# Weighting expert outputs where they are made, and adding them to the residual by DMA, in a two-layer graph attention and mixture-of-experts kernel

## The chip, the cores and the metric

One Trainium2 chip, one of its cores. The metric is the device time of one execution in microseconds, as the median of several runs. In the trace PE is TensorE's matmul, PEld its weight load, DVE is VectorE, ACT is ScalarE, POOL is GpSimd and SP is SyncE; a q behind a name (SPq, ACTq) is that engine's instruction queue.

## The reference

128 graphs of 64 nodes, D = 256, so 8192 tokens. Two layers, each a graph attention and a mixture of 8 experts of which each token uses 2:

```python
# layer 0
x = x + gnn0(layernorm(x), adj)        # Wh = h @ W; e = a1.Wh + a2.Wh; masked softmax; attention @ Wh; elu
t = layernorm(x)
probs = softmax(t @ router_w.T); rw, re = top_k(probs, 2); rw = rw / rw.sum()
x = x + t + sum_k rw[k] * (gelu(t @ w1[re[k]] + b1[re[k]]) @ w2[re[k]] + b2[re[k]])    # hidden 256
# layer 1
x = x + gnn1(layernorm(x), adj)        # the same with a leaky relu ahead of the mask
t = layernorm(x)
vals, idx = top_k(t @ Wg + bg + bias, 2); w = softmax(vals)
x = x + sum_k w[k] * (relu(t @ W1[idx[k]] + b1[idx[k]]) @ W2[idx[k]] + b2[idx[k]])     # hidden 512
```

## The kernel before

Tokens are held in SBUF as `X`, 64 tiles of 128 tokens by 256 values in f32, through both graph layers. Each engine has its program written out in the order in which it runs; waits are on semaphores that count, and a wait holds everything behind it on its engine.

**Graph layer** (both layers). Eight groups g of eight tiles. TensorE turns x (`turn_x`, line 731, a quarter q of a group at a time, two tiles), multiplies by W (`project`, L743) into two banks in turn (2 and 3), builds the edge scores (`edges`, L750, L751), turns the softmax (`turn_probs`, L761) and multiplies by it (`attend`, L771). ScalarE copies the turned x (`copy_xT`, L972), scales the projected rows by 1/std (`scale_rows`, L981), and does the exponentials (L1003, L1019). VectorE does the softmax (`soft`, which starts at L1297), `add_relu` (L1321), `add_exp` (L1328) and the statistics of the result (`second_stats`, L1230), and it prepares group g+2 inside group g. TensorE projects group g+1 inside group g.

**Layer 0's input statistics** are bn_stats (`first_stats`) and a few small steps (`first_norm`); GpSimd takes the inverse root.

**Layer 1's input** is made from layer 0's outputs. GpSimd gathers, for each tile and each of its two choices, the expert's output rows from `yslots` in HBM into a ring (`gather_outputs`, L576, 128 indirect DMAs into `ring0` in WREG; from tile 16 on each pair of tiles waits until TensorE has turned the tile 16 back). VectorE multiplies each by the token's gate and adds it to X (`add_outputs`, L1240, 128 operations, the second with the row sum), and makes the negative mean (L1248). ScalarE makes the sum of squares (`squares`, L997), and VectorE the inverse root (`first_rstd`, L1277 to L1286). In the same groups ScalarE and GpSimd cut layer 1's weights into two f16 parts (L1025, L1026, `low_part` L590).

**Tokens and router.** ScalarE normalises (L1096), VectorE and GpSimd cut the tokens into two f16 halves (L1417, L628), SyncE stores them to HBM: in layer 0 to `split_tokens`, 1024 bytes a row; in layer 1 to `token_rows`, rows of 2056 bytes with tokens, x and two gates. TensorE makes the logits.

**Routing.** VectorE ranks tokens by expert and finds each one's slot. To invert this, it builds one-hot matrices of lane and block for 16 token and choice pairs at a time (L1576 to L1590, `lane_hot`, `block_hot`, the 16 pairs side by side for each lane), and TensorE multiplies them (L890), reading each pair's columns 32 bytes apart. `gather_row` (L1627) is the result, and GpSimd's gathers wait for it. In layer 1 ScalarE then stores the gates at the rows' ends (L1161, 8 bytes for each token). In layer 0 ScalarE adds token and residual meanwhile (x_plus_y, L1138).

**Expert slots.** 256 rows a slot, 68 slots in layer 0 (four of them mixed, with two experts), 2 x 36 in layer 1. In slot s, by engine:

```python
# TensorE                       # ScalarE              # VectorE
output(s)        # L940         activate(s + 2)        cut_hidden(s + 1)   # L1644, L1646
turn_over(s + 3) # L909         # L1149                copy_out(s)         # L1656, waits for output(s)
hidden(s + 2)    # L926                                copy_T(s + 3)       # L1638
```

GpSimd gathers the rows (L640 in layer 0, four slots ahead), and in layer 0 SyncE stores each slot's output to `yslots` when `copy_out` is done. Layer 1 multiplies its outputs by the gate in the slot already (L1669), and its second pass scatters rows to the output (L667). The slots run as a loop of four (layer 0) with the experts' addresses in registers.

## Time and profile before

| | us |
|---|---|
| median of 3 runs | 1438.54 (1426.94 to 1439.29) |
| profiled execution, whole | 1430.36 |
| its span, first to last instruction | 1428.6 |
| busy: TensorE, VectorE, GpSimd, ScalarE | 1123.7, 964.8, 705.0, 551.0 |
| mean granted TensorE clock | 0.856 |

The profile is of one execution. Busy time of an engine says little by itself; what matters is what each stage waits for. By the trace the stages are: graph layer 0 to 186 us, tokens to 240, routing to 296, slots to 538 (layer 0); graph layer to 811, tokens to 862, routing to 930, first pass to 1171, second to the end (layer 1).

### The profile page before, as it was taken

Reading aid. Unit: us, or ns where it says so; the run is one execution under the profiler, and the core shown is the slowest. Engines: PE = TensorE matmul, PEld = TensorE weight load, DVE = VectorE, ACT = ScalarE, POOL = GpSimd, SP = SyncE. Lnnn points to the kernel's source line nnn. Section 1 sums busy time; section 2 is a strip of 40 time slices with the busy share of each in tenths; the row PEclk is TensorE's granted clock in tenths of the full one; section 3 lists DMA queues with packets and bytes.
Section 4 is the critical chain, followed back from the end, with each engine's and each line's share of the span. In section 5 each row is a group of like instructions: output and inputs, shape, how many; then the busy total and the mean of one; then the engine's idle time right before and its main releaser. Section 6 shows DMA issues by size and latency. Waiting matters only on the chain.

```text
span 1428.6 us, 31605 instructions
## 1 busy us (share of the span) xinstructions
PE 1123.7 (79%) x9392; PEld 910.2 (64%) x9393; DVE 964.8 (68%) x1844; ACT 551.0 (39%) x1229; POOL 705.0 (49%) x752
## 2 busy tenths in 40 slices
PE   5988765669999991577667487769999997889995
PEld 4766554348888871355455373549889885668884
DVE  3888688937777762458887797827767664556663
ACT  2646475712222221566766484012222221212221
POOL 3565864045555527756670280045433115677762
PEclk9999855559999995788998658579999998989998
DMA  9211133025555544235452553447766624344430
GB/s 279 55 45 38 60 124 112 1 63 163 162 162 160 165 119 129 85 83 145 123 150 61 147 177 118 3 133 216 201 178 193 147 91 126 111 132 127 124 112 12
DMA packets 126095, 172.53 MB, mean 121 GB/s; under 512 B 35109, under 2 KB 94000, under 8 KB 125744
## 3 DMA queue, kind: packets, MB, share of 16 engines
q0 software_dynamic: 28288, 83.03, 21.9%
q1 hardware_dynamic: 89504, 88.22, 20.0%
q10 hardware_dynamic: 8208, 0.07, 1.0%
q8 instruction: 53, 0.87, 0.3%
q14 instruction: 42, 0.34, 0.1%
HBM read 100.87 MB, written 71.44 MB: 121 GB/s over the span
## 4 chain that ended last, share of the span: by engine, by line
PE 55%; issue 19%; DVE 11%; POOL 6%; ACT 3%; another core or an unknown queue 3%; DMA 2%; DVEq 1%; POOLq 0%; SPq 0%; ACTq 0%
PE bank L926 19%; PE bank L940 19%; PE bank L743 4%; PE bank L909 4%; PE bank L890 3%; DVE X L1240 2%; PE bank L771 2%; POOL arena L628 2%; DVE stats L1230 1%; ACT b_bc L997 1%; PE bank L750 1%; DMA X<-first_rows,gather_row 1%; PE bank L751 1%; DVE X L1321 1%
## 5 line engine op out<-in xcount | busy, mean ns | idle before, releaser
L1149 ACT ACTIVATE arena<-bank,b1T 128x256 f32<-128x256 f32 (+1 forms) x464 | 176.2, 458 | 562.9 <-PE bank L926 363.2
L926 PE MATMUL bank<-arena,WREG 128*128 128x256 f16 (+1 forms) x2784 | 326.5, 270 | 28.2 <-issue 16.6
L940 PE MATMUL bank<-WREG,arena 128*128 x2544 | 304.9, 275 | 21.2 <-issue 13.9
L926 PEld LDWEIGHTS bank<-arena,WREG 128*128 x2784 | 253.8, 99 | 70.7 <-issue 40.4
L940 PEld LDWEIGHTS bank<-WREG,arena 128*128 128x128 f16 x2544 | 246.9, 99 | 61.1 <-issue 29.6
L1644 DVE CAST arena<-arena 128x1024 f16<-128x1024 f32 (+1 forms) x140 | 82.3, 588 | 187.2 <-ACT arena L1149 145.9
L640 POOL DMA_INDIRECT arena<-split_tokens,gather_row x136 | 129.9, 955 | 152.3 <-PE bank L909 64.4
L743 PE MATMUL bank<-wg_sb,arena 128*128 128x258 f32 x512 | 141.6, 423 | 57.6 <-issue 19.7
L576 POOL DMA_INDIRECT WREG<-expert_outputs,pos_both x128 | 126.6, 989 | 91.2 <-issue 35.5
L650 POOL DMA_INDIRECT X<-token_rows,gather_row x72 | 72.5, 1006 | 180.5 <-DMA first_rows<-X 95.9
L743 PEld LDWEIGHTS bank<-wg_sb,arena 128*128 128x128 f32 x512 | 102.4, 209 | 82.4 <-issue 42.6
L1646 DVE TENSOR_TENSOR arena<-arena 128x1024 f16<-128x1024 f32 (+1 forms) x140 | 135.3, 966 | 4.8
L1656 DVE SCALAR_TENSOR_TENSOR arena<-bank,b_bc 128x512 f32<-128x512 f32 (+1 forms) x152 | 97.0, 644 | 37.7 <-PE bank L940 21.3
L1638 DVE COPY arena<-bank 128x1024 f16<-128x1024 f16 x140 | 95.4, 682 | 39.2 <-remote 25.5
L650 POOL DMA_INDIRECT X<-first_rows,gather_row x72 | 76.3, 1060 | 76.8 <-DMA first_rows<-X 47.5
L667 POOL DMA_INDIRECT out<-X,scatter_row x72 | 85.2, 1184 | 58.4 <-DVE X L1669 39.4
L628 POOL TENSOR_TENSOR arena<-arena 128x512 f16<-128x512 f32 x64 | 75.4, 1188 | 44.2 <-DVE arena L1417 44.2
L981 ACT ACTIVATE arena<-bank,minus_one,cols 128x258 f32<-128x258 f32 x128 | 71.1, 565 | 65.7 <-PE bank L743 26.9
L828 PE MATMUL bank<-ident,arena 128*128 128x128 f16 x512 | 65.1, 307 | 37.4 <-POOL arena L628 36.9
L771 PE MATMUL bank<-arena 128*128 128x256 f32 x256 | 73.2, 421 | 25.9 <-DVE X L1321 10.9
L1240 DVE SCALAR_TENSOR_TENSOR X<-WREG,cols,X 128x256 f32<-128x256 f32 x128 | 66.2, 580 | 26.4 <-DMA WREG<-expert_outputs,pos_both 20.6
L771 PEld LDWEIGHTS bank<-arena 128*128 128x128 f32 x256 | 53.3, 214 | 48.1 <-issue 30.2
(205 smaller groups left out, 1577.4 us busy)
## 6 DMA issues: line engine op xcount, KB each, us to landing
first_rows<-X SPq DMA_DIRECT2D x72, 257.0 KB
expert_outputs<-arena SPq DMA_DIRECT2D x68, 256.0 KB
X<-in_x SPq DMA_DIRECT2D x16, 512.0 KB
split_tokens<-arena SPq DMA_DIRECT2D x16, 512.0 KB, 2.9
stage_w<-in_L_ffn_W SPq DMA_DIRECT2D x16, 512.0 KB
token_rows<-X SPq DMA_DIRECT2D x8, 1024.0 KB
token_rows<-arena SPq DMA_DIRECT2D x16, 512.0 KB, 3.8
stage_w<-in_L_ffn_w SPq DMA_DIRECT2D x16, 256.0 KB, 2.7
```

The costliest lines, as they stand in the source:

```text
L576: nc.gpsimd.indirect_dma_start(out=ring0[:, o:o + D], out_offset=None, in_=yslots, in_offset=bass.IndirectOffsetOnAxis(ap=pos_i[k][:, t:t ...
L628: nc.gpsimd.tensor_tensor(y16_4[:, 2 * q:2 * q + 2, D:2 * D], y32_4[:, 2 * (q % 4):2 * (q % 4) + 2, :], y16_4[:, 2 * q:2 * q + 2, 0:D], AL ...
L640: nc.gpsimd.indirect_dma_start(out=gat[:, u * 512:(u + 1) * 512], out_offset=None, in_=table, in_offset=bass.IndirectOffsetOnAxis(ap=gathe ...
L650: nc.gpsimd.indirect_dma_start(out=token_row(ST * j + a, 0, ROW), out_offset=None, in_=first_rows if f else token_rows, in_offset=bass.Ind ...
L743: last = mm(bank[2 + t % 2][:, 0:WA], xT[:, b:b + P], wg(L, c, 0, WA), start=c == 0, stop=c == KC - 1)
L771: last = mm(bank[6 + q % 2][:, a * D:(a + 1) * D], probsT[:, j * P:(j + 1) * P], Wh[g % 2][:, j * WA:j * WA + D], start=True, stop=True)
L926: last = mm(hb, w1_at(L, ea, wh, kc, fc), tT[:, tb:tb + width], start=n == 0, stop=n == 3 * KC - 1)
L940: last = mm(ob[a], hsrc[:, h0:h0 + P], w2_at(L, e[a % len(e)], wh, fc), start=fc == 0 and n == 0, stop=fc == FC - 1 and n == 2)
L1149: ins = A(hid[:, h0:h0 + width], bank[2 + 2 * (u % 2) + fc // 2][:, b0:b0 + width], ACT.Gelu if L == 0 else ACT.Relu, bias=cut(b1T, ea * F ...
L1638: V.tensor_copy(tT[:, (u % 2) * 4 * SLOT:(u % 2 + 1) * 4 * SLOT], bank[u % 2][:].bitcast(F16)).then_inc(T_ev[L], 1)
L1646: tt(hid_lo[:, hb:hb + FC * SLOT], hid[:, hb:hb + FC * SLOT], hid_hi[:, hb:hb + FC * SLOT], ALU.subtract).then_inc(h_split[L], 1)
L1656: ins = stt(o_sb[:, o0:o0 + width].rearrange("p (a d) -> p a d", d=D), bank[6 + u % 2][:, a * width:(a + 1) * width].rearrange("p (a d) -> ...
```

## The change

1. Layer 0's expert outputs are multiplied by their gate in the slot. The gates ride at the end of each token's row: `split_tokens` gets rows of 1032 bytes (256 f32-sized words of token, two gates), ScalarE stores the gates there, and layer 0's gathers wait for that store. In each slot ScalarE picks the gate of the right choice for each row (`pick_gates`) and multiplies the output rows in place (`weigh`); SyncE's store waits for `weigh`.
2. Layer 1's gathers of those outputs go straight to X with `compute_op=add` (`add_choice`), the second choice of a half group after the first has landed; the first choice of half h waits until TensorE has turned half h-4. `add_outputs` and `squares` go. Layer 1's statistics are taken as in layer 0, by bn_stats and `first_norm`, and VectorE's order in the groups becomes that of layer 0.
3. The one-hot matrices hold pairs side by side (two columns, not sixteen), so TensorE reads its columns 4 bytes apart. `gates_ready` comes after the second batch in layer 0 too.
4. The first five tiles of a graph layer are projected into five banks (`FIRST_BANKS`), and ScalarE copies all four quarters of x ahead of the first scaling (in layer 1 the first two quarters, then four scalings).

```diff
-                def gather_outputs(g):
-                    for t in range(g * GT, (g + 1) * GT):
-                        if t >= 2 * GT and t % 2 == 0:
-                            pool.wait_ge(xT_mm[1], at((t - 12) // 2 + 1))
...
+                def add_choice(k, h):
+                    landed = (first_added, both_added)[k][h % 2]
+                    if h >= 2:
+                        pool.wait_ge(landed, 64 * (h // 2))
+                    if k:
+                        pool.wait_ge(first_added[h % 2], 64 * (h // 2 + 1))
+                    elif h >= 4:
+                        pool.wait_ge(xT_mm[1], at(2 * (h - 3)))
+                    for t in range(4 * h, 4 * h + 4):
+                        nc.gpsimd.indirect_dma_start(
+                            out=xs(t), out_offset=None, in_=yslots,
+                            in_offset=bass.IndirectOffsetOnAxis(ap=pos_i[k][:, t:t + 1].bitcast(U32), axis=0),
+                            compute_op=ALU.add).then_inc(landed, 16)
...
+                    pool.wait_ge(x_plus_y[0], at(TILES // 8))
+                    add_choice(0, 0)
                     for g in range(GROUPS):
-                        gather_outputs(g)
+                        for h in range(2 * g, 2 * g + 2):
+                            if h + 1 < 2 * GROUPS:
+                                add_choice(0, h + 1)
+                            add_choice(1, h)
                         if g == 1:
                             one_hot_rows()
...
                 pool.wait_ge(slots_ready[L], at(1))
+                pool.wait_ge(gates_stored, 16 + 16 * L)
...
                     if u % ST == 0 and t >= SV:
                         pool.wait_ge(T_mm[0], at(t // ST - SU + 1))
+                        pool.wait_ge(picks_made, 2 * ST * (t // ST - SU + 1))
...
+                def pick_gates(s, u, i):
+                    def choice(k, a):
+                        return cut(chosen_by[k], ST * s + a, 1)
+                    loop_wait(act, gathered[u % SU], i * (16 * ST) + 16 * ST * (u // SU + 1))
+                    for a in range(ST):
+                        r = u % SU * ST + a
+                        A(part[:, r:r + 1], gathered_row(r, D, 1), ACT.Identity, scale=choice(0, a)).then_inc(picks_made, 1)
+                    for a in range(ST):
+                        r = u % SU * ST + a
+                        loop_wait(act, picks_made, s * (2 * ST) + a + 1)
+                        A(picked[:, r:r + 1], gathered_row(r, D + 1, 1), ACT.Identity, scale=choice(1, a),
+                          bias=part[:, r:r + 1]).then_inc(picks_made, 1)
+                def weigh(s, u):
+                    loop_wait(act, o_ev[0], at(s + 1))
+                    loop_wait(act, picks_made, s * (2 * ST) + 2 * ST)
+                    for a in range(ST):
+                        r = u % SU * ST + a
+                        ins = A(o_sb[:, r * D:(r + 1) * D], o_sb[:, r * D:(r + 1) * D], ACT.Identity, scale=picked[:, r:r + 1])
+                    ins.then_inc(weighted[0], 1)
                 def slot(s, u, i, es):
+                    if L == 0:
+                        weigh(s, u)
                     if u + 2 < SLOTS[L]:
                         activate(s + 2, u + 2, es[2])
+                    if L == 0 and u + 3 < SLOTS[L]:
+                        pick_gates(s + 3, u + 3, i)
...
+FIRST_BANKS = (2, 3, 5, 6, 7)
+        def bank_of(t):
+            return FIRST_BANKS[t] if t < len(FIRST_BANKS) else 2 + t % 2
...
-                    pe.wait_ge(Wh_ev[L], at(t - 1))
+                    if bank_free(t):
+                        pe.wait_ge(Wh_ev[L], at(bank_free(t)))
...
-                        last = mm(bank[2][:, f * nt:f * nt + wide], lane_hot[g % 2].rearrange("p (l t) -> p t l", t=BATCH)[:, b, :],
-                                  block_hot[g % 2][:, 0:wide * BATCH].rearrange("p (l t) -> p t l", t=BATCH)[:, b, :],
+                        last = mm(bank[2][:, f * nt:f * nt + wide], hot(lane_hot[g % 2], P)[:, b // 2, :, b % 2],
+                                  hot(block_hot[g % 2], wide)[:, b // 2, :, b % 2],
```

On VectorE, the order of layer 1's groups:

```diff
                     if g:
-                        add_exp(L, g - 1, 2 + (L == 0))
+                        add_exp(L, g - 1, 3)
                     normalise_probs(L, g)
...
-                            for h in range(2):
-                                add_outputs(g + 2, h)
-                        add_relu(L, g, 0)
-                        add_relu(L, g, 1)
-                        add_exp(L, g, 0)
-                        add_relu(L, g, 2)
-                        add_exp(L, g, 1)
+                    if ahead:
+                        first_stats(L, g + 2, 0)
+                    add_relu(L, g, 0)
+                    add_exp(L, g, 0)
+                    if ahead:
+                        first_stats(L, g + 2, 1)
+                    add_relu(L, g, 1)
+                    add_exp(L, g, 1)
+                    if ahead:
+                        first_norm(L, (g + 2) * GT, GT)
...
+                    add_relu(L, g, 2)
+                    add_exp(L, g, 2)
```

## Rows read from the trace of the kernel before

**Rows 1.** Busy time by stage (stretch, length, engines, granted clock, DMA share, GB/s).

```profile
core 0: us, PE busy (x) PEld busy (x) DVE busy (x) ACT busy (x) POOL busy (x), PEclk, DMA share, GB/s
...
296.00:538.00 242.00, 218.97 (x2224) 192.64 (x2224) 164.91 (x277) 59.60 (x145) 129.67 (x136) 0.95 0.51 149
538.00:811.00 273.00, 160.60 (x800) 117.47 (x800) 184.20 (x489) 152.55 (x371) 148.81 (x138) 0.81 0.41 111
```

**Rows 2.** The same view for 25 slots of layer 0 and one group of layer 1.

```profile
320.00:400.00 80.00, 77.34 (x799) 68.95 (x797) 59.77 (x100) 20.86 (x50) 47.21 (x50) 1.00 0.56 161
655.70:681.50 25.80, 18.92 (x103) 14.35 (x103) 22.96 (x61) 18.34 (x45) 18.00 (x17) 0.93 0.52 143
```

**Rows 3.** Timeline of layer 0's slots, ScalarE and VectorE (start, duration, instruction, idle before).

```profile
403.17 0.84 ACT L1149 ACTIVATE arena<-bank,b1T 128x256 f32<-128x256 f32 x2 [2.10 <-issue]
...
401.78 0.69 DVE L1646 TENSOR_TENSOR arena<-arena 128x512 f16<-128x512 f32 x1
402.39 0.68 DVE L1656 SCALAR_TENSOR_TENSOR arena<-bank,b_bc 128x512 f32<-128x512 f32 x1
...
404.04 0.43 DVE L1644 CAST arena<-arena 128x512 f16<-128x512 f32 x1 [0.37 <-ACT arena L1149]
```

**Rows 4.** Timeline, VectorE: first and last softmax of each layer.

```profile
32.31 0.69 DVE L1297 SCALAR_TENSOR_TENSOR arena<-no_edge,bank 128x512 f32<-128x512 uint8 x1 [10.69 <-PE bank L751]
...
161.34 0.68 DVE L1297 SCALAR_TENSOR_TENSOR arena<-no_edge,bank 128x512 f32<-128x512 uint8 x1
...
594.19 0.69 DVE L1297 SCALAR_TENSOR_TENSOR arena<-no_edge,bank 128x512 f32<-128x512 uint8 x1 [7.78 <-issue]
...
785.95 0.69 DVE L1297 SCALAR_TENSOR_TENSOR arena<-no_edge,bank 128x512 f32<-128x512 uint8 x1 [1.88 <-PE bank L751]
```

**Rows 5.** Groups by line in 655.7 to 681.5 us (count, busy, mean ns, idle before).

```profile
L1240 DVE SCALAR_TENSOR_TENSOR X<-WREG,cols,X 128x256 f32<-128x256 f32 x16 | 8.8, 605 | 0.1
...
L1230 DVE BATCH_NORM_STATS2 stats<-X 128x6 f32<-128x256 f32 x8 | 2.7, 411 | 0.0
...
L997 ACT ACTIVATE b_bc<-X,cols 128x256 f32<-128x256 f32 x8 | 3.9, 496 | 0.0
```

**Rows 6.** Timeline, ScalarE: x_plus_y of layer 0, and the token stage's start in layer 1.

```profile
245.31 31.62 ACT L1138 ACTIVATE X<-X,cols  x64 [0.35 <-issue]
...
811.15 4.04 ACT L1096 ACTIVATE arena<-X,cols 128x256 f32<-128x256 f32 x8 [1.21 <-DVE ex L1404]
```

**Rows 7.** Timeline, start of layer 1: the eighth gather and VectorE's first addition.

```profile
546.76 0.95 POOL L576 DMA_INDIRECT WREG<-expert_outputs,pos_both  x1 [0.30 <-issue]
...
549.60 2.19 DVE L1240 SCALAR_TENSOR_TENSOR X<-WREG,cols,X 128x256 f32<-128x256 f32 x5 [13.54 <-DMA WREG<-expert_outputs,pos_both]
```

**Rows 8.** Single lines: ns min/median/max, first and last start.

```profile
L576 POOL DMA_INDIRECT WREG<-expert_outputs,pos_both x128: 942/948/1372, 538.0 to 745.6; - x128
...
L667 POOL DMA_INDIRECT out<-X,scatter_row x72: 982/1026/1721, 1196.9 to 1419.2; - x72
...
L1240 DVE DVE_READ_ACCUMULATOR X<-WREG,cols,X x64: 78/82/86, 551.7 to 757.4; 128x1 f32 x64
```

**Rows 9.** Groups by line, whole span (count, busy, mean ns, idle before).

```profile
L667 POOL DMA_INDIRECT out<-X,scatter_row x72 | 85.2, 1184 | 58.4 <-DVE X L1669 39.4 <-issue 18.9
...
L1576 DVE TENSOR_TENSOR arena<-arena,lane_of 128x2048 bf16<-128x2048 bf16 x16 | 19.6, 1223 | 5.4 <-PE bank L890 5.3
...
L590 POOL TENSOR_TENSOR WREG<-stage_w,WREG 128x1024 f16<-128x1024 f32 x8 | 17.0, 2131 | 38.7 <-ACT stage_w L1026 38.6
```

**Rows 10.** Routing: matmuls of layer 1, first gather of layer 0, the gates' store.

```profile
907.98 2.43 PE L890 MATMUL bank<-arena 128*128 128x72 bf16 x16 [0.18 <-DVE arena L1583]
911.37 17.32 PE L890 MATMUL bank<-arena 128*128 128x144 bf16 x64 [0.96 <-DVE arena L1590]
...
295.78 1.19 POOL L640 DMA_INDIRECT arena<-split_tokens,gather_row  x1 [63.16 <-DVE gather_row L1627]
...
token_rows<-cols ACTq DMA_DIRECT2D x1, 64.0 KB, 15.3
```

**Rows 11.** Timeline, ScalarE: the first scaling of layer 0.

```profile
19.76 1.02 ACT L981 ACTIVATE arena<-bank,minus_one,cols 128x258 f32<-128x258 f32 x2 [7.92 <-POOL cols L538]
```

More of the change, by code:

```diff
@@ L163, in build @@
         squared = [b2_bc[:, k * D:(k + 1) * D] for k in range(4)]
-        ring0 = WREG[:, 4 * 8 * HID[1]:].bitcast(F32)
+        chosen_by = [stats[:, k * STILES[0]:(k + 1) * STILES[0]] for k in range(TOPK)]
         y32 = carve(8 * D, 0)
@@ L1155, in slot @@
                     if u + 2 < SLOTS[L]:
                         activate(s + 2, u + 2, es[2])
-                if L == 1:
-                    act.wait_ge(gates_ready[1], at(1))
-                    with nc.allow_non_contiguous_dma(reason="two gates at the end of each token's row"):
-                        act.dma_start(rows_of()[:, :, 2 * D:ROW], gates[:].rearrange("p (t k) -> p t k", k=TOPK)).then_inc(gates_stored, 16)
-                act.wait_ge(slots_ready[L], at(1))
+                    if L == 0 and u + 3 < SLOTS[L]:
+                        pick_gates(s + 3, u + 3, i)
@@ L1163, in _ @@
+                act.wait_ge(gates_ready[L], at(1))
+                rows_here, last_column = (rows_of(), 2 * D) if L else (table.rearrange("(t p) c -> p t c", p=P), D)
+                with nc.allow_non_contiguous_dma(reason="two gates at the end of each token's row"):
+                    act.dma_start(rows_here[:, :, last_column:last_column + TOPK], gates[:].rearrange("p (t k) -> p t k", k=TOPK)).then_inc(gates_stored, 16)
+                act.wait_ge(slots_ready[L], at(1 if L else 2))
                 first = of_slots(act, slot_expert, L, phase(0, L, 2), 1)
@@ L1165, in _ @@
                     activate(s, s, first[s])
+                if L == 0:
+                    for s in range(3):
+                        pick_gates(s, s, 0)
                 all_slots(act, L, slot_expert, 1, 2, slot)
@@ L1265, in first_norm @@
                 ch.wait()
-                v, r = (one(n, g * GT, GT) for n in ("var", "rstd"))
+                v, r = (one(name, first, n) for name in ("var", "rstd"))
                 ch.mark(ts(c, c, 1.0 / D, EPS, ALU.mult, ALU.add))
```

222 lines of the change are left out of this document (94 added, 128 removed).

## The prediction

> **What bounds the kernel now.** I read the stage table first [rows 1]. TensorE is busy 218.97 of 242 us in layer 0's expert slots and only 160.60 of 273 in layer 1's graph layer. The change touches both, and the routing of each layer, so each is read by what it waits for.
>
> The slots of layer 0: 80 us hold 799 matmuls at 32 a slot, so 25 slots of 3.2 us, TensorE 77.34 us busy [rows 2]. ScalarE works 0.84 us a slot, then waits for `hidden`. VectorE's order is cast and subtraction (`cut_hidden` of the next slot), `copy_out`, `copy_T` [rows 3].
>
> The graph layer of layer 1: its eight softmaxes start from 594.19 to 785.95, 27.4 us apart on average, against 32.31 to 161.34 in layer 0, 18.4 us [rows 4]. In one group (25.80 us) VectorE is busy 22.96, ScalarE 18.34, GpSimd 18.00, TensorE 18.92 [rows 2]: VectorE is the bound, and its largest row there is `add_outputs`, 8.8 us [rows 5]. VectorE takes group g+2's tokens in its queue inside group g, so late tokens also hold the relu and exp steps queued behind them.
>
> **Part A, weighting in the slots (layer 0).** ScalarE gets, per slot, `weigh` (two 128x256 multiplies in place) ahead of `activate(s+2)`, and `pick_gates(s+3)` (four one-column operations) behind it. It has the room, but the new waits close a ring. `weigh(s)` waits for `copy_out(s)`; `activate(s+2)` is queued behind `weigh(s)`; `cut_hidden(s+2)` waits for `activate(s+2)`; `copy_out(s+1)` is queued behind `cut_hidden(s+2)` on VectorE; `weigh(s+1)` waits for it. One turn is one slot. Its terms: `weigh` 2 x 31.62/64 = 0.99, from layer 0's own x_plus_y of the same shape [rows 6]; `activate` 0.84; to VectorE 0.03 (404.01 to 404.04), and as much back; cast 0.43 and 0.03 to the next; subtraction 0.61 (401.78 to 402.39); `copy_out` 0.68 [rows 3]. Sum 3.64 us; the loop's hop, which falls on every fourth slot, is hidden only in part, so I take 3.75. Against 3.2 that is 0.55 x 64 = 35 us; four mixed slots and the tail (the last store waits for `weigh`) add 2, and the first slots, at half clock, where TensorE is slower than the ring, take 2 off: 35. Low end: `weigh` as short as `activate`'s two, no hop, 3.5, +19. High end: a further 0.1 us at each of the four hand-overs inside the ring, 4.05, +54. `copy_T`, the gathers (four slots ahead) and the stores are off the ring. TensorE then idles 0.5 us a slot; its clock was 1.00 at 97% busy and 0.93 at 73% [rows 2], so a loss from that belongs to the high end. The gathered rows grow from 1024 to 1032 bytes, beside a DMA share of 0.56 [rows 2]: nothing.
>
> **Part B, gathers that accumulate (layer 1).** VectorE loses 8.8 us a group and gains eight bn_stats, 2.7 for eight [rows 5]; the small steps around both about cancel. 6.1 of 22.96 us go, and 3.9 of ScalarE's (`squares`) [rows 5]. VectorE falls under 17, ScalarE to 14, TensorE's 19 stands. What is late next is GpSimd's queue: 16 gathers at 1.25 us and a `low_part` of 2.13 make 22.1 us a group [rows 7, 9]. The stage then follows from that queue: its start at 538.0 [rows 8], 128 gathers at c each, five `low_part` (10.7), `one_hot_rows` about 1, landing 1.9 (the eighth gather ends at 547.7, VectorE starts at 549.60 [rows 7]); then what follows the last tokens: now 757.4 to 811.15, 53.8 us [rows 6, 8], and some 50 with the lighter queues, since the rest of group 5, group 6 and group 7 remain. End = 601.6 + 128 c, against 811.15. The new waits add little: `add_choice(1, h)` waits for transfers issued 4 gathers (5 us) earlier that land in 1.9; the hold by `xT_mm` needs half h-4 turned, and the 16 gathers between that turn and the landing of half h take about as long as the group that lies between. The mean clock was 0.81 in the stage [rows 1], lowest at its beginning, where a slow first group holds the queue; I add 5 us for it.
>
> No row shows c, an accumulating gather. The gather into WREG is 0.95 + 0.30 = 1.25 us [rows 7]; the scatter, the other indirect transfer, has a median of 1.026 and a mean of 1.18, so 1.33 to 1.49 [rows 8, 9]. For less than 1.25 nothing speaks: the issue is the same GpSimd work with one operation more. I take 1.34, since a transfer that also has to read its target is nearer to the scatter. That ends at 773, 38 us earlier, less 5: 33 us. With 1.25 it is 45, with 1.49 14.
>
> The DMA engines: a share of 0.52 over 25.80 us moved 143 GB/s, 3.6 us per MB, so 0.48 us for a gather of 0.131 MB [rows 2]; twice that is still under c, and the sum keeps GpSimd's price. The Trainium skill, "DMA: Bandwidth & Descriptors", section "Rules for kernel authors", says that an accumulating DMA reads its destination and writes it later; a third pass over the bytes by that rule would make some 0.7 of the 0.48, no change of the sum, but it speaks for the rival on this price. No run so far shows such a transfer.
>
> **Part C, routing.** Lanes and blocks lie as pairs, so TensorE reads its moving columns 4 bytes apart and not 32. Now 64 matmuls of 144 columns take 17.32 us and 16 of 72 take 2.43: 0.271 and 0.152 us each, 1.65 ns a column, two cycles at half clock [rows 10]. VectorE waits 5.3 us for them in all [rows 9], and some 2.7 more at the ends of the two chains. If the column price halves, VectorE bounds; its operations keep size and type. In layer 0 the gathers now also wait for the gates' store, which ScalarE issues only after x_plus_y (276.9) and which took 15.3 us [rows 6, 10]: 292.3 against 295.78 now, 3 us at most after one for the new steps. With 3.6 in layer 1 I take 6.6, and 0 or -1 if the stride isn't the reason. The Trainium skill, "SBUF — State Buffer", section "Door 1: The DMA port swizzle", gives SBUF 16-byte lines and a penalty for every access to a new one; by it a 4-byte step is nearly free, which makes the same 6.6. The trace agrees for the 32-byte step, with its 1.65 ns.
>
> **Part D, five banks first.** TensorE can project five tiles before the first `scale_rows`, which starts at 19.76 in layer 0 [rows 11]; today the softmax follows at 32.31, with scaling and projection taking turns. Eight scalings back to back with three projections left save 3 us, or 0 if the next groups absorb it. In layer 1 it is inside the 5 us above.
>
> **Sum.** 35 - 33 - 6.6 - 3 = -7.6 on the profiled execution's 1430.36 us: 1422.8. The median of the three runs lies 8 us above that execution; I carry half of it and predict 1427.
>
> **Rivals.** (1) The accumulating gather is dear, and this one ends slower: c = 1.75. GpSimd's queue then holds the graph layer until 601.6 + 224 = 825.6, 14.5 us later than now, plus 5, plus 35 - 9.6: +45, 1475. It decides from the point where 35 - 9.6 + 5 - (209.6 - 128 c) passes 14 us, c = 1.51. For it: each transfer must fetch its target first; against: the scatter's price is 1.33. (2) The ring doesn't bind, because the weighing or the hand-overs are shorter, or the slots slip past each other: cost 5, total -38, 1393. For it: 3.64 is only 0.44 above the period; against: its terms are measured rows. (3) The change doesn't do what it says: the graph layer's pace stays near 25 us, since another chain through the in-order queues holds it, so B brings 10 and the total is +15, 1446. For it: ScalarE and TensorE idled 7 us a group too; against: VectorE 89% busy, and layer 0's 18.4 us.
>
> **Chances.** Forecast 0.45 (its own range 1400 to 1448, as c goes from 1.25 to 1.49 and the ring from 3.5 to 3.9), dear gather 0.22, no ring 0.19, no gain in the graph layer 0.14. The range 1387 to 1474 takes in rivals 2 and 3 and c up to 1.7. Within 1% (14 us, about what three runs that lie 12 us apart can tell) lie 0.24 of the forecast's share and 0.02 of rival 3's; faster has 0.17 and rival 2's 0.19; slower has the rest.
>
> **What would show it.** In the profile after: slots of 3.7 to 3.8 us in layer 0, with `weigh` waiting for VectorE and the cast waiting for ScalarE; if they keep 3.2, part A's ring is wrong. The start-to-start spacing of the accumulating gathers is c. Softmaxes of layer 1 22 to 25 us apart with GpSimd hardly idle; if they are 18 to 20 apart, GpSimd isn't the bound. Routing batches without VectorE's waits for TensorE. The prediction is wrong above all if c lies outside 1.25 to 1.5, or if the lighter load of TensorE in the slots brings the clock down.

## The result, and the profile after

The changed kernel takes 1486.2 us (median, 1483.1 to 1491.8) beside 1438.1 for the kernel before on the same chip: a ratio of 1.037, 95% interval 1.032 to 1.042, slower. The profiled execution took 1491.78 us (span 1490.0, mean clock 0.854), 61.4 more than that of before.

Both traces, cut at the same marks (the first gather of layer 0's slots, the first gather of expert outputs, the first normalisation of layer 1's tokens, the first gather of layer 1's slots), lengths in us:

| stage | before | after | |
|---|---|---|---|
| up to layer 0's first gather | 295.8 | 288.7 | -7.1 |
| slots of layer 0 | 242.2 | 275.3 | +33.1 |
| graph layer of layer 1 | 273.2 | 304.5 | +31.3 |
| tokens and routing of layer 1 | 119.0 | 114.3 | -4.7 |
| the two passes of layer 1 | 498.5 | 507.3 | +8.8 |

The busy time by stage, as in [rows 1], cut at the marks of after:

```profile
core 0: us, PE busy (x) PEld busy (x) DVE busy (x) ACT busy (x) POOL busy (x), PEclk, DMA share, GB/s
288.70:563.90 275.20, 227.47 (x2224) 188.40 (x2224) 161.54 (x277) 179.71 (x553) 128.73 (x136) 0.97 0.45 132
563.90:868.40 304.50, 166.11 (x800) 120.00 (x800) 148.28 (x392) 122.45 (x243) 220.36 (x138) 0.76 0.55 100
```

In the slots ScalarE rose from 59.60 to 179.71 us, and no engine is full; the granted clock was 0.97, against 0.95 before, so the lighter load of TensorE cost no clock. In the graph layer VectorE fell by 36 us and ScalarE by 30, as meant, but GpSimd rose by 72, and the layer got longer with it.

**The slots.** The ring is the circle of waits between ScalarE and VectorE that part A describes. The timeline that answers to [rows 3], ScalarE and then VectorE. L1191 is `weigh`, L1166 `activate`, L1178 and L1182 the picks, L1675 and L1677 `cut_hidden`, L1687 `copy_out`; an arrow in brackets names what ended the wait:

```profile
423.74 0.91 ACT L1191 ACTIVATE arena<-arena 128x256 f32<-128x256 f32 x2 [1.13 <-DVE arena L1687]
424.55 0.81 ACT L1166 ACTIVATE arena<-bank,b1T 128x256 f32<-128x256 f32 x2
425.26 0.47 ACT L1178 ACTIVATE arena<-arena,stats 128x1 f32<-128x1 f32 x2
425.68 0.66 ACT L1182 ACTIVATE arena<-arena,stats 128x1 f32<-128x1 f32 x2
427.32 0.91 ACT L1191 ACTIVATE arena<-arena 128x256 f32<-128x256 f32 x2 [0.98 <-DVE arena L1687]
...
422.87 0.68 DVE L1687 SCALAR_TENSOR_TENSOR arena<-bank,b_bc 128x512 f32<-128x512 f32 x1
...
425.40 0.43 DVE L1675 CAST arena<-arena 128x512 f16<-128x512 f32 x1 [1.25 <-ACT arena L1166]
425.86 0.69 DVE L1677 TENSOR_TENSOR arena<-arena 128x512 f16<-128x512 f32 x1
426.47 0.68 DVE L1687 SCALAR_TENSOR_TENSOR arena<-bank,b_bc 128x512 f32<-128x512 f32 x1
```

The ring can be walked: `copy_out` starts at 422.87, `weigh` at 423.74 behind it, `activate` at 424.55 behind that, the cast at 425.40, `copy_out` again at 426.47. One turn is 3.60 us; the turns alternate between 3.60 and 3.74, from the third slot to the mixed ones, 3.67 on average over 48 slots. Before, TensorE set them, at 3.07 to 3.45, 3.24 on average. So the ring costs 0.43 x 64 = 28 us of the 33.1. Of the rest, 2.1 us are a pause at 505 us, 1.1 the tail behind the last `copy_out`, and 1.7 the first slots. Both traces have a pause of some 7 us there. In the kernel before it lies ahead of the first `copy_out` (22.1 us behind the stage's first gather, where the other chip below has 15); in the changed kernel it lies between the first `copy_out` and the second, 11.4 us apart, where the run without the hold, on that other chip, has 5.0. The pause itself is thus no price of the change. VectorE's timeline of before, and TensorE's of after, in which the matmuls of one slot come singly:

```profile
308.39 0.69 DVE L1638 COPY arena<-bank 128x1024 f16<-128x1024 f16 x1 [6.50 <-remote]
```

```profile
312.75 0.39 PE L975 MATMUL bank<-WREG,arena 128*128 x2 [1.93 <-issue]
313.35 0.37 PE L975 MATMUL bank<-WREG,arena 128*128 x1 [0.21 <-issue]
314.08 0.38 PE L975 MATMUL bank<-WREG,arena 128*128 x1 [0.36 <-issue]
```

The waits of the stage (total, times, longest) show the ring as well:

```profile
ACT arena L1191 <- DVE arena L1687: 74.0, 66, 4.9
DVE arena L1675 <- ACT arena L1166: 72.2, 57, 2.0
```

**The graph layer.** The accumulating gathers as one line, what GpSimd waited for ahead of them, who waited for them, and their landing:

```profile
L601 POOL DMA_INDIRECT X<-expert_outputs,pos_both x128: 1540/1540/1957, 563.9 to 811.8; - x128
its engine sat idle before it (us, times) until:
  issue: 36.8, 123
  DMA expert_outputs<-arena: 22.8, 1
  DMA X<-expert_outputs,pos_both: 1.2, 4
who waited for it (us, times):
  DVE stats L1278: 139.5, 15
...
DMA to landing us min/median/max: 3.7/3.8/4.6
```

And in GpSimd's timeline, with starts 1.84 to 1.85 us apart:

```profile
573.24 1.54 POOL L601 DMA_INDIRECT X<-expert_outputs,pos_both  x1 [0.30 <-issue]
575.09 1.54 POOL L601 DMA_INDIRECT X<-expert_outputs,pos_both  x1 [0.30 <-issue]
576.93 1.54 POOL L601 DMA_INDIRECT X<-expert_outputs,pos_both  x1 [0.30 <-issue]
```

So c, the prediction's price of one accumulating gather on GpSimd, is 1.54 + 0.30 = 1.845 us by the starts, where the plain gather into WREG had 1.25 [rows 7, 8]. GpSimd waited 1.2 us in all for landings and never for TensorE's turns of the half that is to be overwritten (the hold): it costs nothing here. VectorE's bn_stats waited 139.5 us for the tokens. The softmaxes that answer to the second half of [rows 4] start at 634.87 and 844.30, 29.9 us apart on average, against 27.4:

```profile
634.87 0.69 DVE L1330 SCALAR_TENSOR_TENSOR arena<-no_edge,bank 128x512 f32<-128x512 uint8 x1
...
844.30 0.69 DVE L1330 SCALAR_TENSOR_TENSOR arena<-no_edge,bank 128x512 f32<-128x512 uint8 x1
```

**Routing and first group.** The rows that answer to [rows 10], [rows 11] and the first of [rows 4], in the timelines, and the gates' store in the list of DMA issues:

```profile
961.86 1.14 PE L925 MATMUL bank<-arena 128*128 128x72 bf16 x16 [2.41 <-DVE arena L1609]
...
971.23 2.10 PE L925 MATMUL bank<-arena 128*128 128x144 bf16 x16 [1.28 <-DVE arena L1616]
...
19.20 2.85 ACT L1018 ACTIVATE arena<-bank,minus_one,cols 128x258 f32<-128x258 f32 x6
...
28.53 0.69 DVE L1330 SCALAR_TENSOR_TENSOR arena<-no_edge,bank 128x512 f32<-128x512 uint8 x1 [7.46 <-PE bank L783]
```

```profile
split_tokens<-cols ACTq DMA_DIRECT2D x1, 64.0 KB, 12.8
```

A matmul of 144 columns takes 2.10/16 = 0.131 us, half of the 0.271 of before, and TensorE waits for VectorE between the batches, while VectorE's 5.3 us of waits for these matmuls are gone. Layer 0's first softmax comes 3.8 us earlier, and the scalings ahead of it run six in a row.

### The profile page after: what moved, and what is told of

The parts are those of the page before. It is cut to its first block, busy times and chain, and to the rows that moved or that the text cites. A ratio compares the mean times of both kernels' runs of the same rounds, so it can differ in the third digit from the quotient of the medians.

```text
span 1490.0 us, 32667 instructions
## 1 busy us (share of the span) xinstructions
PE 1107.3 (74%) x9392; PEld 898.8 (60%) x9393; DVE 924.7 (62%) x1750; ACT 640.2 (43%) x1509; POOL 770.0 (52%) x752
## 3 DMA queue, kind: packets, MB, share of 16 engines
q0 software_dynamic: 40576, 83.17, 24.9%
## 4 chain that ended last, share of the span: by engine, by line
PE 33%; issue 25%; POOL 16%; DVE 13%; ACT 4%; DMA 3%; another core or an unknown queue 2%; ACTq 1%; DVEq 1%; SPq 1%; POOLq 0%
PE bank L975 13%; PE bank L961 13%; POOL X L601 10%; DVE arena L1687 3%; ACT arena L1166 2%; PE bank L944 2%; PE bank L775 2%; POOL arena L658 2%; DVE arena L1675 1%; DMA X<-expert_outputs,pos_both 1%; DVE arena L1601 1%; DVE stats L1278 1%; POOL WREG L615 1%; ACT arena L1191 1%
## 5 line engine op out<-in xcount | busy, mean ns | idle before, releaser
L975 PE MATMUL bank<-WREG,arena 128*128 x2544 | 308.3, 274 | 57.0 <-issue 25.8
L1166 ACT ACTIVATE arena<-bank,b1T 128x256 f32<-128x256 f32 (+1 forms) x464 | 174.4, 453 | 408.9 <-PE bank L961 276.2
L975 PEld LDWEIGHTS bank<-WREG,arena 128*128 128x128 f16 x2544 | 241.7, 98 | 110.7 <-issue 82.2
L1675 DVE CAST arena<-arena 128x1024 f16<-128x1024 f32 (+1 forms) x140 | 82.7, 591 | 250.1 <-ACT arena L1166 203.7
L601 POOL DMA_INDIRECT X<-expert_outputs,pos_both x128 | 199.6, 1559 | 60.8 <-issue 36.8
L1278 DVE BATCH_NORM_STATS2 stats<-X 128x6 f32<-128x256 f32 x256 | 87.6, 410 | 140.7 <-DMA X<-expert_outputs,pos_both 139.5
L775 PE MATMUL bank<-wg_sb,arena 128*128 128x258 f32 x512 | 139.5, 419 | 31.5 <-ACT arena L1018 27.8
L1677 DVE TENSOR_TENSOR arena<-arena 128x1024 f16<-128x1024 f32 (+1 forms) x140 | 135.3, 966 | 4.8
L803 PE MATMUL bank<-arena 128*128 128x256 f32 x256 | 76.3, 436 | 46.1 <-DVE X L1354 43.4
L1687 DVE SCALAR_TENSOR_TENSOR arena<-bank,b_bc 128x512 f32<-128x512 f32 (+1 forms) x152 | 96.6, 642 | 17.1 <-remote 11.0
L803 PEld LDWEIGHTS bank<-arena 128*128 128x128 f32 x256 | 53.9, 218 | 70.8 <-issue 60.4
L1191 ACT ACTIVATE arena<-arena 128x256 f32<-128x256 f32 x136 | 61.7, 500 | 75.9 <-DVE arena L1687 74.0
L1048 ACT ACTIVATE arena<-bank,plus_one 128x512 f32<-128x512 f32 x64 | 43.9, 686 | 116.0 <-PE bank L803 112.0
```

The costliest lines, as they stand in the source:

```text
L601: nc.gpsimd.indirect_dma_start(out=xs(t), out_offset=None, in_=yslots, in_offset=bass.IndirectOffsetOnAxis(ap=pos_i[k][:, t:t + 1].bitcast ...
L775: last = mm(Wh_bank(t), xT[:, b:b + P], wg(L, c, 0, WA), start=c == 0, stop=c == KC - 1)
L803: last = mm(bank[6 + q % 2][:, a * D:(a + 1) * D], probsT[:, j * P:(j + 1) * P], Wh[g % 2][:, j * WA:j * WA + D], start=True, stop=True)
L975: last = mm(ob[a], hsrc[:, h0:h0 + P], w2_at(L, e[a % len(e)], wh, fc), start=fc == 0 and n == 0, stop=fc == FC - 1 and n == 2)
L1166: ins = A(hid[:, h0:h0 + width], bank[2 + 2 * (u % 2) + fc // 2][:, b0:b0 + width], ACT.Gelu if L == 0 else ACT.Relu, bias=cut(b1T, ea * F ...
L1278: ch.mark(V.bn_stats(stats[:, t * 6:(t + 1) * 6], xs(t)))
```

## The experiments

The runs came onto several chips, of two kinds: on one kind the kernel before takes 1438 to 1445 us, as in the first pair of traces, on the other 1368 to 1369. I call them the slower and the faster chip and compare within one kind. A difference between two chips of one kind is less sure than one within a chip, and is named where it is used. Stage lengths in us from the profiles, one execution each, cut as above:

| kernel | chip | first gather | slots | graph layer 1 | routing 1 | passes of 1 |
|---|---|---|---|---|---|---|
| before | slower | 295.8 | 242.2 | 273.2 | 119.0 | 498.5 |
| changed | slower | 288.7 | 275.3 | 304.5 | 114.3 | 507.3 |
| changed, again | slower | 289.1 | 277.3 | 302.6 | 115.7 | 509.4 |
| second choice accumulates | slower | 288.0 | 275.8 | 271.5 | 114.0 | 506.5 |
| half rows, half columns | slower | 288.1 | 277.3 | 296.1 | 116.9 | 506.6 |
| activate first, no picks | slower | 288.8 | 247.6 | 304.8 | 114.2 | 510.4 |
| before | faster | 297.6 | 231.9 | 263.0 | 119.0 | 460.0 |
| no hold | faster | 288.2 | 265.8 | 302.9 | 115.6 | 459.4 |
| activate first | faster | 289.4 | 245.4 | 302.8 | 115.6 | 458.6 |
| plain gathers | faster | 287.8 | 265.8 | 230.1 | 114.1 | 456.6 |
| routing and banks | faster | 289.5 | 231.8 | 259.9 | 115.1 | 456.5 |
| routing and banks, again | faster | 288.9 | 232.3 | 258.5 | 115.2 | 457.2 |
| weights in slots, plain sum | faster | 287.6 | 236.0 | 246.0 | 114.4 | 453.7 |
| plain sum without weights in slots | faster | 286.9 | 232.2 | 251.3 | 114.3 | 460.3 |

**1. The order in the slot.**

```diff
+                    if u + 2 < SLOTS[L]:
+                        activate(s + 2, u + 2, es[2])
                     if L == 0:
                         weigh(s, u)
-                    if u + 2 < SLOTS[L]:
-                        activate(s + 2, u + 2, es[2])
```

> The changed kernel, with activate(s+2) ahead of weigh(s) in ScalarE's slot of layer 0. Theory (the ring of weigh, activate, cast, subtraction and copy_out sets 3.65 us a slot): activate no longer stands behind weigh, so the ring is open and a slot goes back to TensorE's 3.2 us; layer 0's slots take some 245 us instead of 275.3, and the whole is 26 to 32 us shorter than the changed kernel, about 1457. Rival (the slots are longer because ScalarE, GpSimd or the transfers of 1032-byte rows have more to do, whatever their order): the slots keep 3.5 us or more, and the whole moves by less than 10 us.

Measured: 1410.8 us, ratio to the kernel before 1.032 (1.025 to 1.038). On this chip the changed kernel stands in the run without the hold (1433.4): 22.6 us less, and 20.4 less in the slots (245.4 against 265.8). The `copy_out`s come no longer evenly but 3.82, 3.77, 3.22, 2.67 us apart, 13.4 for four, where the same chip needs 12.75 without weighting. So the order was most of the price, as the theory said, but 13.5 us stayed against the kernel before on a chip of this kind (231.9). In the steady slots, which hold most of them, one wait of TensorE's comes in four slots, for nothing that the profile shows: 1.03 us here, where the same wait of the kernel before is 0.30. TensorE's timeline:

```profile
409.52 1.47 PE L961 MATMUL bank<-arena,WREG 128*128 128x256 f16 x12
412.02 1.15 PE L975 MATMUL bank<-WREG,arena 128*128 x9 [1.03 <-issue]
```

**2. Without the picks as well.**

```diff
-                        pool.wait_ge(picks_made, 2 * ST * (t // ST - SU + 1))
...
-                    if L == 0 and u + 3 < SLOTS[L]:
-                        pick_gates(s + 3, u + 3, i)
...
-                        ins = A(o_sb..., o_sb..., ACT.Identity, scale=picked[:, r:r + 1])
+                        ins = A(o_sb..., o_sb..., ACT.Identity, scale=plus_one[:])
```

> The changed kernel with activate(s+2) ahead of weigh(s), and without pick_gates: weigh multiplies by 1 in place, so the gates are left out; GpSimd's gathers no longer wait for the picks. With activate first the slots took 13.4 us for four, against 12.7 without any weighting, and TensorE stood still once in four slots for 1.0 us. Theory (ScalarE's slot, 0.84 + 0.90 + 1.0 us with the loop's hop on top, comes late once in four slots, and the picks fill it): without them four slots take 12.7 to 12.9 us, and the whole is 10 us or more below activate first, 32 or more below the changed kernel. Rival (the wait comes from the hand-overs of TensorE itself or of weigh): four slots keep 13.2 us or more.

Measured on the slower chip: 1465.3 us, 28.7 below the changed kernel beside it (1494.0), ratio 1.014 (1.009 to 1.019). Four slots take 13.1 us, where the kernel before needs 12.9 on this chip and the changed one 14.7, so the ring and nearly all of the rest are gone. Both figures missed what I expected, 12.7 to 12.9 and 32 us, which came from the other chip. The picks, four operations on one column, about 1.1 us a slot, were the second part of the price. The edit also takes away the gathers' wait for the picks, so the two are not separated. How they come to hold TensorE once in four slots, the trace doesn't show.

**3. The price of the gather.** The first of two edits of the same line, all gathers plain:

```diff
-                            in_offset=bass.IndirectOffsetOnAxis(ap=pos_i[k][:, t:t + 1].bitcast(U32), axis=0),
-                            compute_op=ALU.add).then_inc(landed, 16)
+                            in_offset=bass.IndirectOffsetOnAxis(ap=pos_i[k][:, t:t + 1].bitcast(U32), axis=0)).then_inc(landed, 16)
```

> The changed kernel, with the 128 gathers of layer 1 as plain gathers into X at the same place, under the same waits: they overwrite X, so the addition to the residual is left out. Theory (the accumulating gather costs GpSimd 1.845 us where a plain one costs 1.25): the spacing falls to 1.25 us, the graph layer of layer 1 to between 225 and 245 us from 304.3, and the whole is 60 to 80 us shorter than the changed kernel, about 1416. Rival 1 (the layer is held by the order, the hold on TensorE's turns, half after half, and by the landing): spacing within a half falls, the layer keeps over 290 us. Rival 2 (the price is that of writing into X at all, 1 KB apart in each partition, not of the accumulation): the spacing stays near 1.8 us.

Measured: 1359.8 us, ratio 0.994 (0.992 to 0.997), 73.7 below the run without the hold. The line of the gathers:

```profile
L601 POOL DMA_INDIRECT X<-expert_outputs,pos_both x128: 942/946/1402, 553.6 to 728.8; - x128
```

The same place in X, the same waits, the same rows: 0.946 us, and the graph layer takes 230.1 where it took 302.9. Both rivals fall: neither the order nor the writing into X is the price, the accumulation is. The prediction's line, 63.6 us (601.6 less its start at 538.0) + 128 c, and its 5 us more for the start, give 228.6 for c = 1.25, 1.5 us under the 230.1 measured.

**4. Half of them.** `compute_op` only where k is 1.

> The changed kernel, in which the first choice's gathers are plain and overwrite X, so the residual is left out, and only the second choice's accumulate. Theory (the graph layer of layer 1 ends with GpSimd's queue, a straight line in the mean price of a gather): the mean is (1.25 + 1.845) / 2 = 1.55 us, so 128 x 0.30 = 38 us are gone from the graph layer, to about 266 us, and the whole is 34 to 40 us below the changed kernel. Rival (each second-choice gather waits for the first choice's landing, or the layer falls at once to the pace of VectorE and TensorE): less than 25, or more than 55 us.

Measured: 1459.6 us, 34.4 below the changed kernel, the graph layer 271.5 us, 31.1 shorter. The mean busy time of its gathers, by the groups of the stage:

```profile
L601 POOL DMA_INDIRECT X<-expert_outputs,pos_both x128 | 165.2, 1291 | 60.7 <-issue 37.4 <-DMA expert_outputs<-arena 22.7 <-PE bank L762 0.6
```

With the 0.30 to the next that is a mean c of 1.59, a little over the 1.55 expected, and 128 x (1.845 - 1.59) = 33 us by the line, 31.1 measured. This kernel's graph layer is about as long as that of before (273.2): part B breaks even there at c = 1.6, and it cost 1.845. On the faster chip, where before's layer takes 263.0, the same line breaks even at 1.52.

**5. What the price depends on.** The first choice's gathers with rows of 512 bytes (L602), the second choice's with 64 rows of 1024 (L607), in one execution.

```diff
+                        if k == 0:
+                            ... out=xs(t)[:, 0:D // 2], in_=yslots.rearrange("r (two c) -> (r two) c", two=2), ...
+                        else:
+                            ... out=xs(t)[0:P // 2, :], ap=pos_i[k][0:P // 2, t:t + 1] ...
```

> The changed kernel with halved accumulating gathers: the first choice's fetch 128 rows of 512 bytes, the second choice's 64 rows of 1024 bytes, so both move half the bytes; half of the expert outputs are left out. Theory (GpSimd's price lies in what it writes for each row): 128 rows of half the width keep 1.54 us busy, 64 whole rows fall to between 0.8 and 1.1. Rival (the price lies in the bytes, in a queue that pushes back): both fall to the same. Second rival (a fixed price of the instruction): both keep over 1.4.

Measured, in GpSimd's timeline:

```profile
592.65 1.54 POOL L602 DMA_INDIRECT X<-expert_outputs,pos_both  x1 [0.30 <-issue]
594.50 1.42 POOL L607 DMA_INDIRECT X<-expert_outputs,pos_both  x1 [0.30 <-issue]
596.22 1.42 POOL L607 DMA_INDIRECT X<-expert_outputs,pos_both  x1 [0.30 <-DMA X<-expert_outputs,pos_both]
```

My theory was wrong: half the bytes cost the same 1.54, as it said, but half the rows 1.42 and not 0.8 to 1.1. The second rival holds. An estimate from the two: 1.9 ns for a row and 1.30 us whatever the size; so a smaller accumulating gather saves next to nothing. The mean c is 1.48 + 0.30 = 1.78, for which the line gives 296.4 us of graph layer with the 5; 296.1 were measured.

**6. Without the hold.**

```diff
-                    elif h >= 4:
-                        pool.wait_ge(xT_mm[1], at(2 * (h - 3)))
```

> The changed kernel without the wait of the first choice's half h for TensorE's turn of half h-4. Theory (GpSimd's queue is the bound and never waits there): no change, within 3 us of the changed kernel. Rival (the hold delays the first choice and so all of the queue): 10 us or more shorter.

Measured on the faster chip: 1433.4 us, ratio 1.047 (1.041 to 1.052), with a graph layer of 302.9 us. The run with `activate` first, on the same chip and with the hold, has 302.8. The hold costs nothing.

The ratio is higher than the changed kernel's 1.037, but the stages don't show it. From the table, the graph layer costs 39.9 us on this chip and 31.3 on the slower one, where before's is 10 us longer and GpSimd's price is not; the passes cost nothing here and 8.8 there; the slots cost 33.9 and 33.1. In sum the spans differ by 60.4 and 61.4 us. The medians differ by 64.3 and 48.0, so the ratio's difference lies between single executions and medians.

**7. The changed kernel again.**

> The changed kernel as it is, so that the next three have it beside them on one chip. Theory: its graph layer of layer 1 takes 303 to 305 us, its slots hold 3.60 to 3.75 us, and it is 55 to 65 us longer than the kernel before; where the two passes of layer 1 took 8.8 us longer in the first profile, with no line of them changed, they now take the same as in the other kernels of the chip.

Measured: 1494.0 us, 48.6 above the kernel before (1445.4), ratio 1.033 (1.028 to 1.038), with a graph layer of 302.6 us. The 55 to 65 was read off two single executions; the first one of before had been 8 us under its median. The graph layer and the ring repeat as expected. The passes of layer 1 did not fall back to those of before: all five traces of changed kernels on this kind of chip have 506.5 to 510.4 us there, the one trace of before 498.5; on the faster chip all kernels have 453.7 to 460.3, before among them with 460.0. So on the slower chip the 8.8 us come back each time, with no line of the passes changed, and on the faster one they are absent. Their cause stays open. What the slower chip has and the faster one lacks are pauses whose releaser the profile calls remote: they stand in each of its traces, of before too, and in none of the faster chip's. Some come at the same place in each, the first slots of layer 0 and the start of each pass, with lengths that vary. First of before, then of after, by the waits of the whole span:

```profile
ACT arena L1149 <- remote: 47.6, 6, 12.0
```

```profile
ACT arena L1166 <- remote: 124.5, 10, 45.4
```

The pauses in the slots named above end with such waits as well (6.50 us of VectorE's before, 3.78 after). What they are, the trace doesn't say.

**8. Routing and banks alone.** The kernel before with part C, and part D in layer 0.

> The kernel before, with the pairwise one-hot matrices of both layers and the five banks and the copies first in layer 0; no weighting in the slots, no accumulating gathers. Theory (these parts gain what the two traces differ by in their stages, 3.8 at layer 0's start, 3.3 less the gates' store in its routing, 4.4 in layer 1's): 8 to 12 us shorter than the kernel before, about 1428. Rival (the differences of single stages come from elsewhere, and the later stages absorb them): within 3 us of the kernel before.

Measured: 1354.6 us, ratio 0.990 (0.987 to 0.992), 14.6 us below before, more than expected.

> The kernel before with pairwise one-hot matrices and layer 0's five banks, once more, so that it stands beside the version above on one chip: 0.9895 of the kernel before, 0.986 to 0.993. If the version above is right, it is 15 to 30 us shorter than this one.

Measured: 1354.7 us, ratio 0.991 (0.988 to 0.994), 15.3 us above the version below (1339.4). Beside it the kernel before was profiled, for its stages:

> The kernel before, for its stages on this chip. Theory: 12.9 to 13.0 us for four slots, its last stage (layer 1's two passes) within 3 us of that of the other two kernels here, so that the 8.8 us by which the first two traces differ there are a difference of runs and not of kernels. Rival: its last stage is 6 us or more shorter than theirs.

Measured: a span of 1371.5 us, its passes 460.0, within 3 us of the 457.2, but 6.3 above the 453.7 of the version below, and four slots in 12.75 us, under the 12.9 to 13.0 expected. Against it this kernel is 8.7 us earlier at the first gather, 4.5 shorter in the graph layer (of which 2.0 are GpSimd's two iotas, 5.2 us before and 3.2 now) and 3.8 in the routing of layer 1.

**9. A version from what was learned.** Plain gathers into the ring, weights in the slots with `activate` first and the picks on VectorE, and half by half one addition for each choice:

```diff
+                    for k in range(TOPK):
+                        o = (c % 4 * TOPK + k) * 4 * D
+                        ins = tt(xs(4 * c, 4), xs(4 * c, 4), ring0[:, o:o + 4 * D], ALU.add)
...
+                    tt(parts, both, cut(chosen_pairs, TOPK * ST * s, TOPK * ST)..., ALU.mult).then_inc(picks_made, 1)
+                    loop_wait(dve, picks_made, s * 2 + 1)
+                    tt(picked[:, r:r + ST], parts[:, :, 0], parts[:, :, 1], ALU.add).then_inc(picks_made, 1)
```

> A version made of what the runs so far showed. From the changed kernel: the weighting in the slots, pairwise one-hot matrices, five banks, bn_stats; with activate(s+2) ahead of weigh(s), and the picks as two small operations on VectorE behind copy_T. In layer 1 the gathers are plain, into the ring of the kernel before, and VectorE adds a half (four tiles, 128x1024) of each choice in one operation, which the weighting makes possible. Theory: four slots take 12.7 to 13.1 us; an addition of 128x1024 takes 1.1 to 1.3 us, four a group, 4.8 in place of 8.8 + 0 for squares, so VectorE has 16.9 + 4.8 = 21.7 us a group beside GpSimd's 22.1; the graph layer of layer 1 falls to 235 to 250 us, and the whole is 28 to 45 us below the kernel before, ratio 0.969 to 0.981. Rival (the stage needs both queues, and late tokens hold the relu and exp steps behind the additions as before): the graph layer keeps over 260 us, ratio 0.985 or more.

Measured: 1339.4 us, ratio 0.980 (0.977 to 0.982): below both kernels and clear of noise, 28.6 us under before. Four slots take 12.97 us, against 12.75; the slots as a whole 3.7 to 4.1 us more than without weighting, where the changed kernel paid 33. The graph layer takes 246.0. But the way there isn't the one expected. Its costliest groups of VectorE between 524 and 790 us:

```profile
L1262 DVE TENSOR_TENSOR X<-X,WREG 128x1024 f32<-128x1024 f32 x32 | 47.3, 1479 | 33.3 <-DMA WREG<-expert_outputs,pos_both 32.8
L1252 DVE BATCH_NORM_STATS2 stats<-X 128x6 f32<-128x256 f32 x128 | 44.1, 412 | 0.6
```

The statistics take 22 us more than before, and VectorE is busy 190.7 us in this stage, more than before's 183.9. ScalarE lost 30.7. The mean of an addition is 1.48 us and not 1.1 to 1.3, but 28 of the 32 took 1.21 to 1.23, as expected. The other four took 1.9, 3.0, 3.1 and 5.1, and each ran beside a `low_part` of GpSimd's (L614). The median, and the longest of them beside GpSimd:

```profile
L1262 DVE TENSOR_TENSOR X<-X,WREG x32: 1206/1225/5095, 535.2 to 717.9; 128x1024 f32<-128x1024 f32 x32
...
707.37 4.21 POOL L614 TENSOR_TENSOR WREG<-stage_w,WREG 128x1024 f16<-128x1024 f32 x2
707.58 5.09 DVE L1262 TENSOR_TENSOR X<-X,WREG 128x1024 f32<-128x1024 f32 x1
```

**10. Which half of it.** The same without weights in the slots, VectorE multiplying tile by tile:

> The version with the plain sum, without the weighting in the slots: no weigh, no picks, rows of 1024 bytes again, and in layer 1 VectorE multiplies by the gate in eight operations of 128x256 a half, as in the kernel before, but with bn_stats, the order of the relu and exp steps and the banks of the changed kernel. It asks where the 12.5 us came from by which the graph layer of the plain sum (246.0 us) was shorter than that of the kernel with routing and banks alone (258.5), since its two wide additions took 1.48 us each and VectorE was busy for 190.7 us, more than the 183.9 before. Theory A (the wide additions: 47.3 us in all against 66.3, and VectorE bounds the stage): the graph layer is 10 to 19 us longer than 246, so 256 to 265, and the whole is 0.985 to 0.992 of the kernel before. Theory B (the row statistics that no longer go through ScalarE, and the order of the queues): the graph layer stays at 243 to 251 us, the slots return to those of the kernel before, and the whole is 0.972 to 0.979, shorter than the version with the weights in the slots.

Measured: 1346.7 us, ratio 0.986 (0.984 to 0.988), slots 232.2, graph layer 251.3, on another chip of the faster kind. Between the theories: of the 12.5 us, 7.2 stay without the wide additions and 5.3 go with them. What made the 7.2, the statistics, the order of the queues or the banks, no run separates. Of the 7.3 us between the spans of this run and the last, 6.6 lie in the passes of layer 1 (460.3 against 453.7), of which no line differs; what that is stays open, and so whether the weights in the slots, which make the wide additions possible (5.3 us), are worth their 3.8 us.

## Why the prediction was wrong

- **The step that failed** is part B's "No row shows c ... I take 1.34": a term of the sum, mis-sized. c measured 1.845, outside its bounds of 1.25 and 1.49, and above even the 1.75 of the first rival, which had a chance of 0.22. The two bounds were the nearest rows, a gather and a scatter, and neither adds; "for less than 1.25 nothing speaks" was reasoned, while for the upper end the scatter's mean simply stood. Put into the prediction's own line, 601.6 + 128 x 1.845 = 837.8, 26.6 later than 811.15; with 5 for the cold start, 35 for the ring and 9.6 off, +57 and 1487, beside 1491.8 for the profiled execution. The 4.4 us between are 8.8 in the passes, which the sum did not have, less 1.9 in the slots, 0.3 of the graph layer and 2.2 of parts C and D.
- **The mechanism was right.** The stage is GpSimd's queue: it follows c at the plain end, in the middle and at the dear end (230.1 us at 1.25 on the faster chip, then 271.5 at 1.59, 296.1 at 1.78, 302.6 and 304.5 at 1.845), within 2.2 us of 68.6 + 128 c. VectorE and ScalarE lost what was said (36 and 30 us). The hold and the waits between the choices cost nothing, as said. By its own line the graph layer breaks even at (811.15 - 601.6 - 5) / 128 = 1.60; the half-way kernel, at 1.59, is 1.7 us under before's. In part the line's constant fits by luck: the 5 us for a slow first group that holds the queue did not come, since GpSimd never waited for TensorE; in their place four `low_part` and `one_hot_rows` took 14.5 us and not 11.7 (five and "about 1"), and 56.6 us and not 53.7 passed from the start of the last gather to the end.
- **Part A, the ring**: 3.64 worked out, 3.75 taken, 3.60 and 3.74 in turn measured; +35 forecast, +33.1 measured, and opened by reordering. The two agree better than their parts: the ring itself cost 28, as before's slots took 3.24 and not 3.2 and the turn 3.67 and not 3.75, and a pause at 505 us, the tail and the first slots made up the rest. The rival without a ring is out. That the picks have a price of their own, 0.16 us a slot with them (3.35 against before's 3.19 on one chip) and 0.04 without (3.28 against 3.24 on the other), was not in the working, which gave ScalarE "the room".
- **Part C**: 6.6 forecast with 3 of it for layer 0; 4.7 in layer 1's routing, and 3.3 in layer 0's (7.1 less part D's 3.8). The column price halved as assumed. The gates' store took 12.8 us and did not hold the first gather, which waited for VectorE: it was issued at 268.8, while `x_plus_y` was still running, and not after it, as the prediction had it.
- **Part D**: 3 forecast, 3.8 measured.
- **The DMA side.** The accumulating transfers land 3.8 us after their issue, plain ones of the same rows 2.8 (both medians, the latter from experiment 3), and the queue's packets rise from 28288 to 40576; yet in its stage the DMA share is 0.55, and the landing was covered by the gathers of the other choice's half that are issued between. It was the instruction's own time on GpSimd, and not the traffic, that set c, as the gathers of half the bytes show. The Trainium skill, "DMA: Bandwidth & Descriptors", section "Rules for kernel authors", says that such a DMA reads its destination and writes it later; the longer landing agrees.
- The Trainium skill, "DMA: Bandwidth & Descriptors", section "SWDGE vs HWDGE vs iDMA", leaves accumulation to GpSimd's DMAs, so by it the work could not go to SyncE's queue; no run here tried that.

## What to carry to other kernels

Before work is moved into a DMA's option (accumulate, cast, scatter), have one row of exactly that instruction on its issuing engine: here the option cost GpSimd 0.6 us for each of 128 issues and saved VectorE 0.55 us each (less the new bn_stats), and GpSimd was the next bound already. If no row exists, the upper bound is not the nearest other instruction; work out from which price the change loses, and give the side beyond it the chance that an unknown deserves. In a loop where every engine runs in order, put the step that feeds the next stage ahead of the step that waits for the last one: one swap of two calls was worth 20 us of the 34 that the slots had grown by.

## What the runs showed of the hardware that was not expected

- An accumulating indirect gather holds GpSimd for 1.54 us at 128 rows, whether of 512 or 1024 bytes, and 1.42 at 64 rows; a plain one of 128 rows 0.946. It lands 3.8 us after its issue, the plain one 2.8.
- Worked out from the packet counts, each accumulated row went as a packet of its own and plain rows four to a packet. The changed kernel has 12288 packets more than that with plain gathers (28288), three quarters of its 16384 rows; with half of the gathers accumulating there are 34432, and with the halved ones 36480, as the same rule gives:

```profile
q0 software_dynamic: 40576, 83.17, 24.9%
```

- Chips of two kinds run the same kernel in 1438 to 1445 and in 1368 us. A ring of hand-overs between ScalarE and VectorE took 3.60 to 3.75 us on both; what differs is TensorE's slots (12.94 against 12.75 us for four), the graph layer of layer 1 (273.2 against 263.0) and above all the passes of layer 1 (498.5 against 460.0).
- VectorE's additions of two SBUF tiles took far longer beside GpSimd's `low_part`: in the kernel before 2.5 us four times and 4.6 once, where the median is 0.48, in the version of experiment 9 up to 5.1 where it is 1.225.
- Reading a bf16 moving matrix with a step of 32 bytes between columns cost 0.271 us for 144 columns, with a step of 4 bytes 0.131, both at a granted clock of 0.50 (1.2 GHz). The step of the weights that are loaded for it changed in the same edit.
- Four ScalarE operations on a single column take 1.1 us together, more than two on 256 columns (0.9); the same picks take VectorE two operations of 0.15.
